# Eight instead of six products by C on GpSimd in a Mamba block with a ternary feed-forward layer, and the steps around them

## The chip, the cores and the metric

One NeuronCore of a Trainium2 chip runs the whole program. The metric is the device time of one execution in microseconds; lower is better. Engines are named as the profile names them: PE is TensorE, DVE is VectorE, ACT is ScalarE, POOL is GpSimd, and SP is the sync engine, which only issues transfers here.

## What is computed

Sixteen rows (the batch) of 512 tokens with 256 channels pass through a selective scan, a layer norm, a feed-forward net and a second layer norm. The part that matters:

```python
xx, res = split(x @ in_w.T)               # 512 inner channels each
xx = silu(causal_conv4(xx) + conv_b)
delta, B, C = split(xx @ xproj_w.T)       # 16 states
delta = softplus(delta @ dt_w.T + dt_b)
dA, dBu = exp(delta * A), delta * B * u
carry = dA[t] * carry + dBu[t]            # the scan over 512 tokens
y[t] = sum over 16 states of carry * C[t]
x1 = layernorm(x + ((y + u * D) * silu(res)) @ out_w.T)
h = silu(x1 @ w1) * (x1 @ w2)
h = gelu(h @ h1); h = gelu(h @ h2)
out = layernorm(x1 + h @ w3)
```

## The kernel before

The channels lie on the 128 partitions in four tiles (DC = 4), the 512 tokens of a row along the free axis. A row has 16 states times 4 channel tiles = 64 scan tiles. Two tiles make a **pair**, so a row has 32 pairs, numbered p = 0 to 31; pair p belongs to state p // 2.

Each engine runs its own list of instructions in order, and semaphores tie the lists together. The order is written by hand as **steps**: one iteration of the main loop has 64 steps s = 0 to 63, and in iteration i four rows are in flight at once: row i is scanned, row i+1 goes through its *front* (input projection, convolution, delta), row i-1 through its *tail* (gates, output projection, first norm, first feed-forward layer, and the hidden layers from step 31 on), and row i-2 through its *end* (the rest of the hidden layers at steps numbered 64 and up, the last layer, second norm, output). Constants at the head of the file say in which step each thing is issued: `T_RES`, `T_GATE`, `T_OUT`, `T_ADD`, `T_STATS` for the tail, `E_W3`, `E_SCALE`, `E_ADD`, `E_STATS` for the end, `F_...` for the front, `B_AT` for the transposes that PE makes for a pair, `HALF_AT`, `GELU_AT` and `SPLIT_AT` for half matrix products, GELUs and splits of the hidden layers, `L1_AT` for the tiles of the first layer, and `EXP_COUNT` for how many tiles of exp(delta * A) ACT makes in a step. A step is no time: engines meet only where a semaphore makes them.

For a pair, PE transposes dB = duT * B into PSUM (`b_pair`, L420). DVE scans at step 2p (`scan_pair`, L792). At step 2p+1 the states are multiplied by C and stored in one of four buffers hC. For most pairs DVE does that from PSUM (`c_pair`, L803). For pairs in `POOL_PAIRS` (rows 1 to 15) or `FIRST_POOL_PAIRS` (row 0), the scan writes hC itself and POOL multiplies in place (`y_pair`, L991); GpSimd has no part in the scan. Then POOL issues the transfer that adds hC to y (L1001). These transfers go in two chains, for even and odd pairs, and each waits for the one before it in its chain. The C rows are loaded by SP for a state at a time into two buffers (`load_c`), when the products two states back are done.

PE starts `b_pair` of pair p when PSUM of pair p-2 is free: after the product by C where DVE makes it, already after the scan where POOL does.

The feed-forward products use a high and a low part: POOL splits each activation tile into both (`split_tile`, L1040 and L1042). The tail's gates are L710 on ACT and L887 on DVE; the sum with x is L894, the scaling of the last layer L923, its sum with x1 L930, and the first layer's gate and product L908 and L915.

Of the kernel before, what the change touches and what calls it, by code (L numbers as in the profile page):

```python
# [37 lines left out]
QUARTERS = 2 * W3_SLOTS  # L38


T_RES = (0, 6, 7, 9)
T_GATE = (2, 5, 8, 11)
T_OUT = (12, 14, 16, 17)
T_ADD = (16, 18)
T_STATS = (17, 18)
T_NORM = 19
T_X1T = (20, 21)
E_W3 = (10, 11, 12, 18)
E_SCALE = (12, 19)
E_ADD = (14, 20)  # L50
E_STATS = (17, 21)
E_NORM = 22
B_AT = (-2, 0, 4, 5, 7, 9, 10, 12, 14, 15, 18, 20, 22, 24, 26, 28, 31, 32, 34, 35, 37, 40, 42, 43, 47, 48, 50, 51,
        54, 56, 58, 61)
L1_AT = (22, 24, 25, 26, 27, 28, 29, 31)
L1_SPLIT_AT = (22, 24, 25, 26, 27, 28, 29, 30)
HALF_AT = (31, 32, 34, 35, 36, 37, 38, 40, 42, 44, 45, 46, 47, 48, 49, 50, 51, 52, 53, 54, 55, 56, 57, 60, 61, 62,
           63, 64, 65, 70, 71, 72)
GELU_AT = (38, 39, 39, 45, 46, 47, 49, 51, 56, 57, 57, 65, 65, 66, 72, 72)
SPLIT_AT = (39, 40, 41, 47, 48, 49, 51, 52, 60, 61, 62, 66, 69, 70, 72, 72)  # L60
F_XX = (30, 32, 34, 36)
FIRST_XX = (30, 31, 32, 33)
F_DBL = 39
F_DBL_OUT = 40
F_BT = 48
F_BT_OUT = 51
F_DT = (40, 41, 43, 46)
F_PLUS = (44, 46, 47, 49)
F_BASE = (41, 43, 46, 50)
F_LOST = (47, 47, 49, 51)  # L70
F_LN = 51
F_DELTA = (53, 53, 53, 53)
F_DELTA_U = (53, 53, 53, 53)
F_Y = (59, 59, 61, 63)
F_DU = (55, 56, 57, 58)
F_XR = 51
SCALE_LEAD = 7

EXP_LEAD, DA_RING = 4, 8
EXP_COUNT = (1, 2, 0, 0, 2, 0, 3, 1, 0, 1, 0, 0, 0, 3, 1, 0, 0, 4, 0, 1, 3, 0, 0, 1, 2, 0, 2, 1, 0, 0, 2, 0, 1, 2,
             1, 0, 2, 3, 1, 0, 2, 1, 3, 0, 1, 0, 0, 0, 3, 2, 0, 0, 0, 2, 3, 0, 0, 0, 1, 0, 0, 2, 3, 1)
EXP_FIRST = EXP_LEAD
EXP_AT = [(EXP_FIRST + sum(EXP_COUNT[:s]), EXP_COUNT[s]) for s in range(TILES)]
PREP_AT = (-30, -27, -25, -24, -20, -12, -7, -5, -3, 2, 5, 12, 16, 17, 18, 20, 23, 26, 30, 33, 38, 39)
# [3 lines left out]
FLAG_AT = 48  # L90
DVE_SLOTS = 12
X_FRONT_AT = 22
OUT_AT = 24
X32 = 4
RAW = 4
HC_SLOTS = 4
POOL_PAIRS = (1, 8, 11, 13, 16, 17)
FIRST_POOL_PAIRS = (0, 3, 4, 9, 14, 16, 17, 18, 25, 27, 28)
SUM_AT = tuple(min(63, 2 * p + (5 if p in FIRST_POOL_PAIRS else 3)) for p in range(0, PAIRS, 2))

# [21 lines left out]
def build(nc, x, xT_in, in_wT, chan, xproj_wT, dt_wT, out_wT, ffn_w, ffn_s, w3_s, ident_in, out):  # L122
# [3 lines left out]
    with ExitStack() as ctx:  # L126
# [171 lines left out]
        def _(sp):  # L298
# [42 lines left out]
            def entry_step(e):  # L341

                used = e - RING
                if used < 0:
                    return E_W3[-1]
                if used < FIRST_HALF:
                    return L1_AT[used]
                return HALF_AT[used - FIRST_HALF]

# [64 lines left out]
        def _(pe):  # L414
# [80 lines left out]
            def tail_step(r, par, s):  # L495
                if s in T_RES:
                    c = T_RES.index(s)
                    if c:
# [7 lines left out]
                    in_proj(misc_ps, DC + c, xT_tail).then_inc(pe_res, 1)  # L506
                if s in T_OUT:
                    t = T_OUT.index(s)
                    if t == 0:
# [82 lines left out]
            def iteration(i, par, full):  # L592
                (scan, _), (front, fpar), (tail, tpar), (end, _) = rows(i, par)
                for s in range(TILES):
                    if scan is not None and s in B_AT:
                        b_pair(scan, B_AT.index(s))
                    if front is not None and s - TILES in B_AT:
                        b_pair(front, B_AT.index(s - TILES))
                    if i == 0 and s in SUM_AT:
                        sum_pair(2 * SUM_AT.index(s))  # L600
                    if i == 0 and s == FLAG_AT + 1:
                        pe.wait_ge(low_summed, 1)
                        nc.tensor.matmul(ffn_ps[0][0:1, 0:1], low_sum[:], ones[:], start=True, stop=True
                                         ).then_inc(low_total, 1)
                    if end is not None and s in E_W3:
                        w3_tile(end, E_W3.index(s), full)
                    if tail is not None:
# [6 lines left out]
                    if tail is not None:  # L614
                        if s in L1_AT:
                            l1_tile(tail, L1_AT.index(s), full)
                        if s in HALF_AT:
                            half_tile(tail, HALF_AT.index(s), full)

# [12 lines left out]
        def _(act):  # L632
# [71 lines left out]
            def tail_step(r, s):  # L704
                if s in T_GATE:
                    c = T_GATE.index(s)
                    act.wait_ge(pe_res, r * DC + (c + 1))
# [52 lines left out]
        def _(dve):  # L760
# [122 lines left out]
            def tail_step(r, par, s):  # L883
                if s in T_GATE:
                    c = T_GATE.index(s)
                    dve.wait_ge(v_tanh, r * DC + (c + 1))
# [32 lines left out]
            def end_step(f, par, s):  # L919
                if s in E_SCALE:  # L920
                    k = E_SCALE.index(s)
                    dve.wait_ge(pe_w3, f * TT + 2 * (k + 1))
# [3 lines left out]
                                            ).then_inc(w3_scaled, 1)  # L926
                if s in E_ADD:
                    k = E_ADD.index(s)
                    dve.wait_ge(w3_scaled, f * 2 + (k + 1))
                    nc.vector.tensor_tensor(out_st[:, 2 * k:2 * k + 2, :], out_st[:, 2 * k:2 * k + 2, :],  # L930
                                            x1[:, par, 2 * k:2 * k + 2, :], ALU.add).then_inc(z2_ready, 1)
                if s in E_STATS:
                    statistics(1, out_st, f, E_STATS.index(s), z2_ready)
                if s == E_NORM:
# [47 lines left out]
        def _(pool):  # L982
# [69 lines left out]
            def iteration(i, par):  # L1052
                (scan, spar), (front, fpar), (tail, tpar), (end, _) = rows(i, par)
                for s in range(TILES):
                    if scan is not None and s % 2:
                        y_pair(scan, spar, s // 2)
                    if tail is not None:
                        if s - 1 in T_GATE:
                            gate_tile(tail, tpar, T_GATE.index(s - 1))
                        if s == T_STATS[-1]:  # L1060
                            rstd_of(0, tail)
                        ffn_step(tail, s)
                    if end is not None:
                        if s == E_STATS[-1]:
                            rstd_of(1, end)
# [62 lines left out]
```

## Time and profile before

| what | value |
| --- | --- |
| median of 3 runs | 2681.95 us (2679.81 to 2683.85) |
| the profiled execution | 2681.34 us |
| its span in the trace | 2679.5 us |
| DVE busy | 2413.4 us, 90% of the span |
| PE busy | 2423.5 us, 90% (ends are modelled) |
| ACT busy | 2101.1 us, 78% |
| POOL busy | 1605.8 us, 60% |

The 1.84 us between span and time lie around the program. Matrix products overlap in PE's pipeline, so PE's busy share is not its share of peak speed. In the middle of the run the iterations follow each other at an even pace, so a difference in one iteration counts as often as it repeats. In a timeline row, the bracket at the end says how long the engine stood idle before the instruction, and which engine's work ended that; a row without bracket began as soon as its engine was free.

### The profile page before, as it was taken

To read this page: it belongs to the slowest core of one execution; us is meant where nothing else is said; L and a number is where in the kernel's file an instruction comes from. 1 tells how busy PE (TensorE), PEld (TensorE's weight loads), DVE (VectorE), ACT (ScalarE), POOL (GpSimd) and SP (SyncE) were. 2 spreads that over 40 slices of the span, in tenths; PEclk is the share of its full clock that TensorE was granted. 3 is DMA by queue.
4 is the path that set the end of the run, shared out by engine and by line. 5 is a ranking of instruction groups with operands and counts; after the bars stand their busy time and mean duration, and the time that the engine had idled before them with its cause. 6 is when DMAs were issued, how large, how long until landed. Compare 5 with 4: busy or idle time off the path is not lost. (4 is left out here: it accounts for less than half of the span.)

```text
span 2679.5 us, 36236 instructions
## 1 busy us (share of the span) xinstructions
PE 2423.5 (90%) x12098; PEld 1844.0 (69%) x12098; DVE 2413.4 (90%) x2388; ACT 2101.1 (78%) x3225; POOL 1605.8 (60%) x1561
## 2 busy tenths in 40 slices
PE   5677999989999998989999899998989899898988
PEld 2445776867767686776767677686767768576777
DVE  6899999999999999999999999999999999999730
ACT  5886988969788896978879697887969789696611
POOL 1335567665756666566566656656665675657554
PEclk7889999999999999999999999999999999999999
DMA  7758999989899898989989898998989899898933
GB/s 250 217 138 197 223 216 223 228 211 237 206 225 225 214 231 209 238 204 223 223 219 232 206 236 200 228 224 213 243 205 229 204 231 223 212 241 201 254 105 114
DMA packets 224491, 573.26 MB, mean 214 GB/s; under 512 B 25664, under 2 KB 26048, under 8 KB 223824
## 3 DMA queue, kind: packets, MB, share of 16 engines
q0 software_dynamic: 71424, 260.08, 51.9%
q1 hardware_dynamic: 152880, 310.84, 35.3%
q8 instruction: 99, 1.62, 0.2%
q14 instruction: 88, 0.72, 0.1%
HBM read 301.86 MB, written 20.45 MB: 120 GB/s over the span
## 5 line engine op out<-in xcount | busy, mean ns | idle before, releaser
L792 DVE TENSOR_TENSOR_SCAN scan_ps<-dA,scan_ps 128x1024 f32<-128x1024 f32 x411 | 939.7, 2286 | 62.4 <-PE scan_ps L420 61.5
L1001 POOL DMA_DIRECT2D y<-hC x496 | 441.6, 890 | 714.8 <-DVE hC L803 544.6
L651 ACT ACTIVATE dB<-duT,bT 128x512 f32<-128x512 f32 x1024 | 711.0, 712 | 50.9 <-PE scan_ps L420 50.8
L539 PE MATMUL ffn_ps<-hb_hi,ring 128*128 128x512 f32 x1536 | 655.2, 427 | 36.5 <-DVE gate L908 17.4
L642 ACT ACTIVATE dA<-delta,ch 128x512 f32<-128x512 f32 (+1 forms) x1024 | 681.3, 711 | 0.9
L420 PE MATMUL scan_ps<-ident,dB 128*128 128x128 f32 x4096 | 556.7, 282 | 76.8 <-DVE hC L803 60.9
L420 PEld LDWEIGHTS scan_ps<-ident,dB 128*128 128x128 f32 x4096 | 488.1, 145 | 193.7 <-issue 67.2
L539 PE MATMUL ffn_ps<-hb_lo,ring 128*128 128x512 f32 x1536 | 611.2, 398 | 0.0
L803 DVE TENSOR_TENSOR hC<-scan_ps,c_rows_sb 128x1024 f32<-128x1024 f32 x411 | 501.0, 1219 | 42.6 <-DMA c_rows_sb<-c_rows 5.7
L539 PE MATMUL ffn_ps<-ha_hi,ring 128*128 128x512 f32 x1024 | 428.0, 418 | 25.9 <-POOL ha_lo L1042 25.7
L539 PE MATMUL ffn_ps<-ha_lo,ring 128*128 128x512 f32 x1024 | 402.5, 393 | 0.0
L539 PEld LDWEIGHTS ffn_ps<-hb_hi,ring 128*128 128x128 f32 x1536 | 295.6, 192 | 131.7 <-DVE gate L908 39.1
L1042 POOL TENSOR_TENSOR ha_lo<-x,ha_hi 128x512 fp32r<-128x512 f32 x256 | 329.1, 1285 | 21.2
L539 PEld LDWEIGHTS ffn_ps<-hb_lo,ring 128*128 128x128 f32 x1536 | 296.2, 193 | 63.8 <-issue 10.7
L991 POOL TENSOR_TENSOR hC<-hC,c_rows_sb 128x1024 f32<-128x1024 f32 x101 | 252.5, 2500 | 70.0 <-DVE hC L792 69.9
L539 PEld LDWEIGHTS ffn_ps<-ha_hi,ring 128*128 128x128 f32 x1024 | 193.2, 189 | 112.9 <-issue 38.5
L1040 POOL CAST ha_hi<-x 128x512 fp32r<-128x512 f32 x256 | 195.0, 762 | 109.3 <-DVE x L915 93.1
L719 ACT ACTIVATE x<-ffn_ps,fs 128x512 f32<-128x512 f32 x256 | 170.0, 687 | 83.8 <-PE ffn_ps L539 82.7
L792 DVE TENSOR_TENSOR_SCAN hC<-dA,scan_ps 128x1024 f32<-128x1024 f32 x101 | 229.8, 2277 | 3.3 <-ACT dA L642 3.3
L539 PEld LDWEIGHTS ffn_ps<-ha_lo,ring 128*128 128x128 f32 x1024 | 193.9, 189 | 41.8 <-issue 6.7
L728 ACT ACTIVATE gate<-ffn_ps,fs 128x512 f32<-128x512 f32 x128 | 87.8, 686 | 150.5 <-PE ffn_ps L539 150.5
L1042 POOL TENSOR_TENSOR hb_lo<-x,hb_hi 128x512 fp32r<-128x512 f32 x128 | 168.3, 1315 | 10.6
(103 smaller groups left out, 3172.2 us busy)
## 6 DMA issues: line engine op xcount, KB each, us to landing
y<-hC POOLq DMA_DIRECT2D x496, 512.0 KB, 6.3
ring<-rounded_weights SPq DMA_DIRECT2D x704, 256.0 KB, 4.9
c_rows_sb<-c_rows SPq DMA_DIRECT2D x256, 256.0 KB, 5.0
x<-ffn_w SPq DMA_DIRECT2D x22, 512.0 KB, 6.1
rounded_weights<-ffn_w SPq DMA_DIRECT2D x22, 512.0 KB, 6.4
xt<-x_chan SPq DMA_DIRECT2D x16, 512.0 KB, 3.9
xt<-x_tok SPq DMA_DIRECT2D x16, 512.0 KB, 5.5
out_st<-x_chan SPq DMA_DIRECT2D x16, 512.0 KB, 4.9
```

Of the source, the lines that this page charges most:

```text
L420: mm = nc.tensor.transpose(dst[:, j * P:(j + 1) * P], src(j), ident[:])
L539: mm = nc.tensor.matmul(dst, w, a, start=(first and n == 0), stop=(last and n == len(steps) - 1))
L642: nc.scalar.activation(dA[:, s % DA_RING, s % 2:], delta2[:, par, c, s % 2:], ACT.Exp, scale=a_neg[:, c, n:n + 1]).then_inc(dA_ready, 1)
L651: nc.scalar.activation(dB[:, n % 2, t, :], duT[:, t, :], ACT.Copy, scale=bT2[:, par, t, n:n + 1]).then_inc(dB_ready, 1)
L719: nc.scalar.activation(x32[:, i % X32, :], ffn_ps[(2 * HC + i) % 3][:], ACT.Gelu, scale=fs[:, 2 + i // HC, i % HC:i % HC + 1]).then_inc(ge ...
L728: nc.scalar.activation(gate[:, o % 2, :], ffn_ps[2 * o % 3][:], ACT.Tanh, scale=s1_half[:, o:o + 1]).then_inc(l1_tanh, 1)
L792: nc.vector.tensor_tensor_scan(states, dA[:, a:a + 2, :].rearrange("p a l -> p (a l)"), b, 0.0, ALU.mult, ALU.add).then_inc(scan_done, 1)
L803: nc.vector.tensor_tensor(hC[:, (r * PAIRS + p) % HC_SLOTS], scan_ps[:, h:h + 2, :], c_rows[:, n % 2].unsqueeze(1).to_broadcast([P, 2, SEQ ...
L991: nc.gpsimd.tensor_tensor(hC[:, slot], hC[:, slot], c_rows[:, n % 2].unsqueeze(1).to_broadcast([P, 2, SEQ]), ALU.mult).then_inc(hC_pool, 1)
L1001: pool.dma_start(y2[:, par, c:c + 2, :], hC[:, slot], accum_op=ALU.add).then_inc(y_added[p % 2], 16)
L1040: nc.gpsimd.tensor_copy(hi[:, i % HC, :], x32[:, i % X32, :]).then_inc(ffn_hi, 1)
L1042: nc.gpsimd.tensor_tensor(lo[:, i % HC, :], x32[:, i % X32, :], hi[:, i % HC, :].bitcast(F32), ALU.subtract).then_inc(ffn_lo, 1)
```

## The change

`POOL_PAIRS` gains pairs 7 and 10, so in rows 1 to 15 POOL makes eight products by C of 32 instead of six. Beside that, 16 tables of steps change: several entries by one or two steps, `F_PLUS[0]` and `E_STATS[0]` by two, `F_Y` by up to four, and `EXP_COUNT` as a whole (its sum stays 64). No function changes.

```diff
-T_RES = (0, 6, 7, 9)
-T_GATE = (2, 5, 8, 11)
-T_OUT = (12, 14, 16, 17)
+T_RES = (0, 5, 7, 9)
+T_GATE = (2, 5, 8, 10)
+T_OUT = (13, 14, 15, 16)
-E_W3 = (10, 11, 12, 18)
-E_SCALE = (12, 19)
-E_ADD = (14, 20)
-E_STATS = (17, 21)
+E_W3 = (10, 12, 13, 18)
+E_SCALE = (13, 19)
+E_ADD = (15, 20)
+E_STATS = (15, 21)
-B_AT = (-2, 0, 4, 5, 7, 9, 10, 12, 14, 15, 18, 20, 22, 24, 26, 28, 31, 32, 34, 35, 37, 40, 42, 43, 47, 48, 50, 51,
+B_AT = (-2, 0, 3, 5, 7, 8, 10, 12, 14, 15, 18, 20, 22, 25, 26, 28, 31, 32, 34, 35, 37, 40, 41, 42, 47, 48, 50, 51,
         54, 56, 58, 61)
-L1_AT = (22, 24, 25, 26, 27, 28, 29, 31)
+L1_AT = (23, 24, 25, 26, 27, 28, 30, 31)
-HALF_AT = (31, 32, 34, 35, 36, 37, 38, 40, 42, 44, 45, 46, 47, 48, 49, 50, 51, 52, 53, 54, 55, 56, 57, 60, 61, 62,
-           63, 64, 65, 70, 71, 72)
-GELU_AT = (38, 39, 39, 45, 46, 47, 49, 51, 56, 57, 57, 65, 65, 66, 72, 72)
-SPLIT_AT = (39, 40, 41, 47, 48, 49, 51, 52, 60, 61, 62, 66, 69, 70, 72, 72)
+HALF_AT = (31, 32, 34, 35, 36, 37, 38, 40, 41, 44, 45, 46, 47, 48, 49, 50, 51, 52, 53, 54, 55, 56, 57, 59, 61, 62,
+           63, 66, 67, 70, 71, 72)
+GELU_AT = (38, 39, 39, 45, 47, 47, 49, 50, 56, 57, 57, 65, 65, 66, 72, 73)
+SPLIT_AT = (38, 40, 40, 48, 48, 50, 51, 51, 57, 58, 63, 66, 68, 70, 71, 72)
-F_BT_OUT = 51
-F_DT = (40, 41, 43, 46)
-F_PLUS = (44, 46, 47, 49)
-F_BASE = (41, 43, 46, 50)
-F_LOST = (47, 47, 49, 51)
-F_LN = 51
-F_DELTA = (53, 53, 53, 53)
-F_DELTA_U = (53, 53, 53, 53)
-F_Y = (59, 59, 61, 63)
-F_DU = (55, 56, 57, 58)
+F_BT_OUT = 49
+F_DT = (40, 41, 43, 47)
+F_PLUS = (42, 45, 46, 49)
+F_BASE = (41, 44, 45, 49)
+F_LOST = (45, 47, 49, 51)
+F_LN = 52
+F_DELTA = (54, 54, 54, 54)
+F_DELTA_U = (54, 54, 54, 54)
+F_Y = (55, 56, 60, 62)
+F_DU = (55, 56, 57, 59)
-EXP_COUNT = (1, 2, 0, 0, 2, 0, 3, 1, 0, 1, 0, 0, 0, 3, 1, 0, 0, 4, 0, 1, 3, 0, 0, 1, 2, 0, 2, 1, 0, 0, 2, 0, 1, 2,
-             1, 0, 2, 3, 1, 0, 2, 1, 3, 0, 1, 0, 0, 0, 3, 2, 0, 0, 0, 2, 3, 0, 0, 0, 1, 0, 0, 2, 3, 1)
+EXP_COUNT = (0, 3, 0, 0, 2, 0, 1, 2, 2, 0, 0, 2, 1, 2, 1, 0, 0, 0, 2, 1, 4, 0, 0, 0, 3, 1, 0, 1, 0, 2, 1, 0, 1, 0,
+             3, 0, 3, 1, 2, 0, 2, 1, 2, 1, 0, 0, 0, 0, 0, 5, 0, 0, 0, 1, 4, 0, 0, 0, 2, 0, 2, 0, 0, 3)
-OUT_AT = 24
+OUT_AT = 26
-POOL_PAIRS = (1, 8, 11, 13, 16, 17)
+POOL_PAIRS = (1, 7, 8, 10, 11, 13, 16, 17)
```

## Rows read from the trace of the kernel before

**Rows 1.** The page: busy time, share of the span, number of instructions.

```profile
PE 2423.5 (90%) x12098; PEld 1844.0 (69%) x12098; DVE 2413.4 (90%) x2388; ACT 2101.1 (78%) x3225; POOL 1605.8 (60%) x1561
```

**Rows 2.** One iteration's window: busy us of each engine, granted clock, DMA share.

```profile
2219.00:2376.35 157.35, 146.96 (x753) 112.80 (x752) 150.19 (x149) 131.26 (x202) 100.31 (x98) 0.99 0.92 221
```

**Rows 3.** DVE's timeline: the same instruction in two iterations (start, us, instruction).

```profile
1112.45 2.49 DVE L855 TENSOR_TENSOR du<-y,delta 128x512 f32<-128x512 f32 x4
...
1269.82 2.48 DVE L855 TENSOR_TENSOR du<-y,delta 128x512 f32<-128x512 f32 x4
```

**Rows 4.** DVE's timeline, same iteration: waits that end at PE or ACT.

```profile
1142.27 2.30 DVE L792 TENSOR_TENSOR_SCAN scan_ps<-dA,scan_ps 128x1024 f32<-128x1024 f32 x1 [0.78 <-PE scan_ps L420]
...
1146.34 0.69 DVE L887 SCALAR_TENSOR_TENSOR gate<-gate,misc_ps 128x512 f32<-128x512 f32 x1 [0.42 <-ACT gate L710]
...
1242.58 2.30 DVE L792 TENSOR_TENSOR_SCAN scan_ps<-dA,scan_ps 128x1024 f32<-128x1024 f32 x1 [1.51 <-PE scan_ps L420]
```

**Rows 5.** PE's timeline, same iteration.

```profile
1168.02 3.62 PE L514 MATMUL ffn_ps<-outw,y 128*128 128x256 f32 x16
...
1175.85 1.09 PE L420 MATMUL scan_ps<-ident,dB 128*128 128x128 f32 x8 [1.43 <-DVE hC L803]
...
1215.19 0.50 PE L539 MATMUL ffn_ps<-ha_hi,ring 128*128 128x512 f32 x1 [1.52 <-POOL ha_lo L1042]
```

**Rows 6.** Groups by line: busy us, mean ns; idle before and releasers.

```profile
L803 DVE TENSOR_TENSOR hC<-scan_ps,c_rows_sb 128x1024 f32<-128x1024 f32 x411 | 501.0, 1219 | 42.6 <-DMA c_rows_sb<-c_rows 5.7 <-DMA y<-hC 4.3 <-DVE scan_ps L792 1.0
L991 POOL TENSOR_TENSOR hC<-hC,c_rows_sb 128x1024 f32<-128x1024 f32 x101 | 252.5, 2500 | 70.0 <-DVE hC L792 69.9
```

**Rows 7.** DVE's timeline around pairs 7 and 10.

```profile
1164.75 0.67 DVE L930 TENSOR_TENSOR out_st<-out_st,x 128x512 f32<-128x512 f32 x1
1165.35 1.21 DVE L803 TENSOR_TENSOR hC<-scan_ps,c_rows_sb 128x1024 f32<-128x1024 f32 x1
1166.47 2.27 DVE L792 TENSOR_TENSOR_SCAN hC<-dA,scan_ps 128x1024 f32<-128x1024 f32 x1
...
1172.75 0.68 DVE L894 TENSOR_TENSOR xt<-ffn_ps,xt 128x512 f32<-128x512 f32 x1
...
1175.71 0.68 DVE L923 TENSOR_TENSOR out_st<-ffn_ps,w3s 128x512 f32<-128x512 f32 x1
...
1180.98 1.21 DVE L803 TENSOR_TENSOR hC<-scan_ps,c_rows_sb 128x1024 f32<-128x1024 f32 x1
1182.11 0.74 DVE L869 BATCH_NORM_STATS2 stats<-out_st 128x6 f32<-128x256 f32 x2
```

**Rows 8.** POOL's timeline, same iteration.

```profile
1166.86 0.87 POOL L1001 DMA_DIRECT2D y<-hC  x1 [3.03 <-DVE hC L803]
...
1176.46 0.98 POOL L1001 DMA_DIRECT2D y<-hC  x1 [0.38 <-DMA y<-hC]
1182.49 0.85 POOL L1001 DMA_DIRECT2D y<-hC  x1 [5.05 <-DVE hC L803]
...
1213.18 0.61 POOL L1040 CAST ha_hi<-x 128x512 fp32r<-128x512 f32 x1 [1.73 <-DVE x L915]
...
1220.31 2.76 POOL L991 TENSOR_TENSOR hC<-hC,c_rows_sb 128x1024 f32<-128x1024 f32 x1 [0.74 <-DVE hC L792]
...
1291.53 1.29 POOL L1042 TENSOR_TENSOR ha_lo<-x,ha_hi 128x512 fp32r<-128x512 f32 x1
```

**Rows 9.** DVE's timeline: a pair of POOL's, and an operation beside POOL's.

```profile
1217.94 2.28 DVE L792 TENSOR_TENSOR_SCAN hC<-dA,scan_ps 128x1024 f32<-128x1024 f32 x1
1220.13 0.67 DVE L824 SCALAR_TENSOR_TENSOR y<-delta,y 128x512 f32<-128x512 f32 x1
...
1291.58 1.53 DVE L861 TENSOR_SCALAR y<-y,ch 128x512 f32<-128x512 f32 x1
```

**Rows 10.** One line's instructions: durations in ns, lowest, median, highest.

```profile
L861 DVE TENSOR_SCALAR y<-y,ch x64: 473/479/1545, 49.3 to 2394.0; 128x512 f32<-128x512 f32 x64
```

## The prediction

> **What bounds the kernel now.** I read the page first, for shares: DVE and PE are both at 90%, ACT at 78%, POOL at 60% [rows 1]. Two engines at 90% don't say which one sets the pace, so I went on to one iteration. In DVE's timeline the same instruction returns after 1269.82 - 1112.45 = 157.37 us [rows 3], and in a window of that length DVE is busy for 150.2 us, PE for 147.0, ACT for 131.3, POOL for 100.3, the transfers for 0.92 of the time at a granted clock of 0.99 [rows 2]. So an iteration has 7 us in which DVE isn't computing and 10 in which PE isn't; no engine bounds it by itself. The time is a cycle that runs through several, and the reader has to find where it passes from one to the next. I took the timelines of all four engines for one iteration and looked for idle times.
>
> DVE waits for PE or ACT only from step 42 on, and at the start of the next iteration: 1.51 us at the scan of pair 22, 0.78 at that of pair 2, 0.42 at the second gate [rows 4]. From the second gate at 1146.34 to the scan of pair 21 it has no bracket: there its own work is the path. PE has the opposite picture. Its waits lie between 1175.85 and 1215.19, the last of 1.52 us on a split of POOL's [rows 5], which had itself stood idle for DVE's product of the first layer (L915) [rows 8]. After that PE runs on with one wait of half a microsecond until the third part of the output projection and the last part of w3 in the next iteration. So the cycle is: DVE from the second gate to the last tile of the first layer, 67 us; POOL's split; PE through the hidden layers; ACT, which in the same stretch has no idle time until it makes that gate, for which DVE waits the 0.42 [rows 4]; and DVE again. Work taken from DVE between 1146 and 1213 shortens the cycle; work taken elsewhere needn't.
>
> **The change part by part.**
>
> *The products of pairs 7 and 10.* Both lie within that stretch. From the start of the product of pair 7 to the next start DVE spends 1166.47 - 1165.35 = 1.12 us, and for pair 10 1182.11 - 1180.98 = 1.13 [rows 7]. That is 2.25 us an iteration (the mean duration of 1.219 [rows 6] counts an overlap of 0.1 with the next instruction twice). It happens in the scans of rows 1 to 15: 15 x 2.25 = 33.8 us.
>
> *What POOL takes over.* Two products of 2.50 us [rows 6] and about 0.3 until the transfer can be issued: 5.6 us on an engine that is idle for 57. Where they fall: for pair 7, POOL stood idle for 3.03 us before the transfer at 1166.86, for pair 10 5.05 before the one at 1182.49 [rows 8]. The second hides entirely. The first ends about 1 us later than the old product did, at about 1167.9, and the odd chain of transfers with it: the one of pair 9 already waited 0.38 for that of pair 7 [rows 8], so it goes to about 1177.4. Behind it stand POOL's product of pair 10 (its scan ends at 1178.8 then) and, behind that, the second norm's root, needed by DVE at about 1184.1 and done by 1183.8. So 0.3 us is left of that cover; if the landing is 1 us later still, it costs DVE 0.7. I take 0, with 0.7 as the other end. SP's load of C for pairs 12 and 13 waits for pair 9 as before, that for 10 and 11 now for POOL, 1 us later than the 1166.5 at which DVE was done with pair 7, and 11 us ahead of its use; ring loads stand behind it, and none was urgent there.
>
> *PE's side of the same pairs.* `b_pair` of pairs 9 and 12 now waits for a scan, not a product. That only helps: a wait on the product of pair 10 goes. `b_pair` of pair 11 stood 1.43 us for the product of pair 9 [rows 5], which is earlier by pair 7's 1.12. Here is the limit of the gain: PE ends the third and fourth part of the output projection at 1171.64 and DVE uses them at 1172.75; the last part of w3 ends near 1174.4 and DVE takes it at 1175.71 [rows 5, 7]. The slack is 1.1 to 1.3 us, and taking out pair 7 uses 1.12 of it. So the product of pair 7 may give its 1.12 in full, with nothing over.
>
> *Moved steps on DVE in this stretch.* `E_SCALE` to 13 puts the product of pair 6 directly behind its scan, `L1_AT[6]` to 30 puts work between scan and product of pair 15. A product right behind its scan starts 2.42 us after the scan's start, other work 2.20: +0.22 and -0.22. `E_STATS` to 15 puts statistics right behind their sum, about +0.1 from the same pattern (starts 0.70 apart rather than 0.58). `T_GATE[3]` a step earlier finds ACT ready by 0.5 us. Sum 0.1, so 2.15 from DVE.
>
> *Moved steps on PE and ACT.* `b_pair` 22 passes the second delta projection, and takes up to 1.05 of DVE's wait of 1.51; `b_pair` 2 passes a half product of 1.85 and takes the 0.78 [rows 4]. Both waits lie outside DVE's part of the cycle: the second gate is still made by ACT at the same place, so they turn into a longer wait there. The fourth delta projection goes behind a half product, which gives ACT its GELU up to 1.05 earlier and the exponential behind it 0.2 later; ACT's chain to the gate gains 0 to 1.0. Against that, `F_PLUS[0]` at 42 comes before ACT's exponential is done (0.6 of wait), `F_DELTA` behind a scan of 2.3 us uses up most of the 1.9 us that PE's transposes had, and the new `EXP_COUNT` has one to two tiles more lead where DVE's old lead was none (steps 12, 16 and 60), one where it had four (48). Tables and work counts stay equal. I take +0.1 us of gain, with -1.5 and +2.3 (both of DVE's waits on PE in full) as the ends. The same moves in iterations -1, 0, 16 and 17 I take as 0, with 3 us to either side.
>
> *A shared resource.* DVE operations on data in SBUF and POOL's operations slow each other: L861 took 1.53 us when it began beside POOL's L1042, against a median of 0.48 [rows 8 to 10], so it waited until POOL was done. In the new order `E_ADD` (L930) comes right behind the scans of both new pairs, and POOL's product starts when the scan ends. The nearest row is pair 17: DVE's next operation began 2.19 us after the scan's start, POOL's product 2.37 after it and took 2.76 instead of the median of 2.4: DVE was first and POOL paid [rows 8, 9]. I take 0 for DVE, and 0.4 on POOL.
>
> The Trainium skill, SBUF — State Buffer, section Who interferes with whom, says that a DVE instruction with two SBUF inputs and a GpSimd one that reads SBUF take one port in turn, and that whichever starts first keeps it for the whole instruction. The trace agrees (1.53 against 0.48). Its page Perfetto Trace Analysis, section Optimizing Scalar/DVE Operations, warns that moving work between these two engines might not help. By that rule at its worst the sum would be that of the third rival below. The scan and the products that go have one input in PSUM, and by the first page they don't contend.
>
> *Sum.* 2.15 + 0.1 = 2.25 us in each of 15 iterations, 33.8 us. From the profiled execution's 2681.34 that makes 2647.6; the median of the runs is 0.6 above it, so 2648.
>
> **The rivals.**
>
> *More (2614 to 2640).* PE's and ACT's new order shortens their part of the cycle as well. For it speaks that the two waits on PE, 2.29 us, are just where `b_pair` moved. Against it, the output projection's slack of 1.1 is used up. In full 15 x (2.25 + 2.3) = 68 us: 2614.
>
> *Less (2658 to 2676).* PE's chain doesn't follow: DVE arrives 1.1 us earlier at the output projection and finds it late, or transfers of the odd chain hold POOL. Then only pair 10 pays, 15 x 1.13 = 17 us: 2665. For it speaks the small slack, and 0.92 of transfer time that becomes 0.94.
>
> *Slower.* POOL's product takes the port before L930. L930 then waits for the whole product, 2.4 us. For one pair that is 2.4 - 2.25, +2 us in all; for both 4.8 - 2.25 = 2.55 an iteration, 38 us: 2720. It is decided by 0.18 us, the distance of 2.37 and 2.19; should POOL see the end of the scan earlier than DVE can start its next instruction, it goes this way.
>
> *No change (2676.6 to 2687.3).* The products go from DVE, but what they leave is wait: the cycle closes through PE alone. Against it: PE is idle for 10 us an iteration, and all of that hangs on DVE.
>
> **How the numbers follow.** The forecast, 2640 to 2658, gets 0.48; more 0.16; less 0.23; no change 0.05; slower 0.08. Two in a thousand of the time, 5.4 us, is what a measurement of this kernel can tell from nothing, since the runs shown spread over 4 us. So faster is 0.87, the same 0.05, slower 0.08. The range of 2626 to 2671 takes in the forecast, most of "less", which reaches past the 2665 of one pair alone, and the upper part of "more".
>
> **What the profile after should show.** L803 x381 and L991 x131; 147.9 us of DVE in a window of an iteration; L855 returning after 155.1 us; pair 7's gap on DVE closed, with L930 at 0.67 and POOL's product at up to 2.8; DVE's wait at the scan of pair 22 under 0.5, and a longer one at the second gate; PE's 1.43 before `b_pair` 11 nearly gone. I'm wrong if L930 takes over 1 us, if DVE waits at L894 or L923 for PE, or if the return time is under 154 or over 156.

## The result and the profile after

The changed kernel takes 2709.36 us (median of 4 runs, 2706.68 to 2711.5) beside 2680.89 for the kernel before in the same job: ratio 1.0105, 95% interval 1.0092 to 1.0118. It is 28 us slower where 34 us of gain were forecast. The profiled execution took 2711.5 us, its span 2709.7.

The page of the changed kernel, busy time of the engines [rows 1]:

```profile
PE 2429.5 (90%) x12098; PEld 1839.3 (68%) x12098; DVE 2390.9 (88%) x2358; ACT 2111.3 (78%) x3225; POOL 1689.7 (62%) x1591
```

Its groups of the two products [rows 6]:

```profile
L803 DVE TENSOR_TENSOR hC<-scan_ps,c_rows_sb 128x1024 f32<-128x1024 f32 x381 | 464.4, 1219 | 33.9 <-DMA c_rows_sb<-c_rows 6.9 <-DMA y<-hC 3.9 <-DVE scan_ps L792 1.0
...
L991 POOL TENSOR_TENSOR hC<-hC,c_rows_sb 128x1024 f32<-128x1024 f32 x131 | 337.1, 2574 | 107.3 <-DVE hC L792 97.9 <-DMA c_rows_sb<-c_rows 8.5 <-DMA y<-hC 0.7
```

The work went where it should: 30 products of 1.219 us left DVE, 36.6 us. But DVE's busy time fell by only 22.5, so other instructions of DVE take more. DVE's timeline, the same instruction in two iterations [rows 3]:

```profile
1130.44 0.69 DVE L855 TENSOR_TENSOR du<-y,delta 128x512 f32<-128x512 f32 x1
...
1290.55 0.69 DVE L855 TENSOR_TENSOR du<-y,delta 128x512 f32<-128x512 f32 x1
```

This iteration takes 160.1 us instead of 157.4. It is one of the longer ones: from the third iteration on the changed kernel's last 158.5 to 160.7 us, 159.8 in the mean of 13, against 157.5 before. That is 2.3 us each and 30 in all, which is the difference between the two profiled executions. I split the iteration at the second gate and at PE's first half product behind the last first-layer tile. DVE's part, second gate to the start of the last L915, went from 65.93 us (1212.27 - 1146.34) to 64.3 to 64.8: it gained 1.2 to 1.6, not 2.15. The rest of the cycle, PE's half products to the next second gate, went from 88.5 to between 91.2 and 93.0. The loss is there, and the reader finds where it starts in the timelines around step 49. DVE of the changed kernel:

```profile
1228.51 0.75 DVE L915 SCALAR_TENSOR_TENSOR x<-gate,fs,ffn_ps 128x512 f32<-128x512 f32 x1
...
1269.62 2.30 DVE L792 TENSOR_TENSOR_SCAN scan_ps<-dA,scan_ps 128x1024 f32<-128x1024 f32 x1 [1.38 <-PE scan_ps L420]
1272.05 1.23 DVE L803 TENSOR_TENSOR hC<-scan_ps,c_rows_sb 128x1024 f32<-128x1024 f32 x1
1274.57 2.05 DVE L838 TENSOR_SCALAR out_st<-du 128x512 f32<-128x512 f32 x1 [1.30 <-PE misc_ps L475]
1276.55 1.78 DVE L844 SCALAR_TENSOR_TENSOR delta<-gate,delta 128x512 f32<-128x512 f32 x1
```

The same stretch of the kernel before:

```profile
1254.18 2.29 DVE L792 TENSOR_TENSOR_SCAN scan_ps<-dA,scan_ps 128x1024 f32<-128x1024 f32 x1 [0.75 <-PE scan_ps L420]
1256.61 1.23 DVE L803 TENSOR_TENSOR hC<-scan_ps,c_rows_sb 128x1024 f32<-128x1024 f32 x1
1257.87 0.43 DVE L838 TENSOR_SCALAR out_st<-du 128x512 f32<-128x512 f32 x1
1258.21 0.69 DVE L844 SCALAR_TENSOR_TENSOR delta<-gate,delta 128x512 f32<-128x512 f32 x1
```

And POOL of the changed kernel at that moment:

```profile
1273.58 0.88 POOL L1001 DMA_DIRECT2D y<-hC  x1 [0.86 <-DVE hC L803]
1274.19 1.59 POOL L1009 TENSOR_TENSOR delta<-delta,du 128x512 f32<-128x512 f32 x1
1275.43 0.90 POOL L1040 CAST hb_hi<-x 128x512 fp32r<-128x512 f32 x1
1276.41 1.36 POOL L1042 TENSOR_TENSOR hb_lo<-x,hb_hi 128x512 fp32r<-128x512 f32 x1
1282.18 0.88 POOL L1001 DMA_DIRECT2D y<-hC  x1 [4.41 <-DVE hC L803]
1282.78 0.90 POOL L1040 CAST hb_hi<-x 128x512 fp32r<-128x512 f32 x1
```

Step 49 holds the product of pair 24 (L803) and then the fourth "1 + e" of the softplus (L838); L844 is the softplus step behind it. DVE comes to L838 after a wait of 1.30 us for PE's transposes L475. By then POOL has begun its base step (L1009, its own part of the softplus), its split follows, and L838 and L844 take 2.05 + 1.78 us instead of 0.43 + 0.69: 2.71 us more for the same work. DVE's next product comes later by that, POOL's transfer waits 4.41 us for it with the next two splits queued behind it, and PE waits for those. PE's timeline:

```profile
1281.94 1.09 PE L420 MATMUL scan_ps<-ident,dB 128*128 128x128 f32 x8 [0.90 <-DVE hC L803]
...
1287.01 0.50 PE L539 MATMUL ffn_ps<-hb_hi,ring 128*128 128x512 f32 x1 [2.13 <-POOL hb_lo L1042]
```

In the waits of the whole run, PE's L539 stood 37.8 us for `hb_lo`, against 14.0 before, both times in 16 waits. This reading is only a chain of neighbours in time until something in it is taken out. The total of PE's wait alone turns out to be a poor measure of the loss: two runs below have the one without the other.

### The profile page after: what moved, and what is told of

Same layout as the page of the kernel before. It is cut to its first block and busy times, and to the rows that moved or that the text cites. A ratio compares the mean times of both kernels' runs of the same rounds, so it can differ in the third digit from the quotient of the medians.

```text
span 2709.7 us, 36236 instructions
## 1 busy us (share of the span) xinstructions
PE 2429.5 (90%) x12098; PEld 1839.3 (68%) x12098; DVE 2390.9 (88%) x2358; ACT 2111.3 (78%) x3225; POOL 1689.7 (62%) x1591
## 5 line engine op out<-in xcount | busy, mean ns | idle before, releaser
L792 DVE TENSOR_TENSOR_SCAN scan_ps<-dA,scan_ps 128x1024 f32<-128x1024 f32 x381 | 871.2, 2287 | 66.9 <-PE scan_ps L420 48.1
L539 PE MATMUL ffn_ps<-hb_hi,ring 128*128 128x512 f32 x1536 | 667.4, 435 | 69.8 <-POOL hb_lo L1042 37.8
L420 PE MATMUL scan_ps<-ident,dB 128*128 128x128 f32 x4096 | 550.4, 279 | 72.0 <-DVE hC L803 56.6
L539 PE MATMUL ffn_ps<-hb_lo,ring 128*128 128x512 f32 x1536 | 614.8, 400 | 0.0
L420 PEld LDWEIGHTS scan_ps<-ident,dB 128*128 128x128 f32 x4096 | 484.0, 143 | 177.7 <-DVE hC L803 54.4
L803 DVE TENSOR_TENSOR hC<-scan_ps,c_rows_sb 128x1024 f32<-128x1024 f32 x381 | 464.4, 1219 | 33.9 <-DMA c_rows_sb<-c_rows 6.9
L539 PE MATMUL ffn_ps<-ha_hi,ring 128*128 128x512 f32 x1024 | 427.5, 417 | 28.0 <-POOL ha_lo L1042 25.6
L539 PEld LDWEIGHTS ffn_ps<-hb_hi,ring 128*128 128x128 f32 x1536 | 297.5, 194 | 171.7 <-DVE gate L908 52.9
L991 POOL TENSOR_TENSOR hC<-hC,c_rows_sb 128x1024 f32<-128x1024 f32 x131 | 337.1, 2574 | 107.3 <-DVE hC L792 97.9
L539 PE MATMUL ffn_ps<-ha_lo,ring 128*128 128x512 f32 x1024 | 401.7, 392 | 0.0
L539 PEld LDWEIGHTS ffn_ps<-hb_lo,ring 128*128 128x128 f32 x1536 | 298.0, 194 | 66.5 <-issue 14.1
L792 DVE TENSOR_TENSOR_SCAN hC<-dA,scan_ps 128x1024 f32<-128x1024 f32 x131 | 298.3, 2278 | 5.3 <-PE scan_ps L420 5.3
L539 PEld LDWEIGHTS ffn_ps<-ha_hi,ring 128*128 128x128 f32 x1024 | 192.3, 188 | 131.7 <-issue 39.5
L539 PEld LDWEIGHTS ffn_ps<-ha_lo,ring 128*128 128x128 f32 x1024 | 193.0, 188 | 41.9 <-issue 6.7
```

The lines of the kernel that those rows point to most:

```text
L420: mm = nc.tensor.transpose(dst[:, j * P:(j + 1) * P], src(j), ident[:])
L539: mm = nc.tensor.matmul(dst, w, a, start=(first and n == 0), stop=(last and n == len(steps) - 1))
L792: nc.vector.tensor_tensor_scan(states, dA[:, a:a + 2, :].rearrange("p a l -> p (a l)"), b, 0.0, ALU.mult, ALU.add).then_inc(scan_done, 1)
L803: nc.vector.tensor_tensor(hC[:, (r * PAIRS + p) % HC_SLOTS], scan_ps[:, h:h + 2, :], c_rows[:, n % 2].unsqueeze(1).to_broadcast([P, 2, SEQ ...
L991: nc.gpsimd.tensor_tensor(hC[:, slot], hC[:, slot], c_rows[:, n % 2].unsqueeze(1).to_broadcast([P, 2, SEQ]), ALU.mult).then_inc(hC_pool, 1)
```

## The experiments

Each ratio is to the kernel before on the same chip; its 95% interval stands behind it.

**Pairs without moves.** The kernel before with

```diff
-POOL_PAIRS = (1, 8, 11, 13, 16, 17)
+POOL_PAIRS = (1, 7, 8, 10, 11, 13, 16, 17)
```

> The kernel before with the new POOL_PAIRS alone; all step tables as before. Theory A (the moved steps cost the time, the two products on GpSimd gain it): the stretch from the second gate to the last first-layer tile shrinks by 1.6 to 2.2 us an iteration as in the profile after, nothing else changes, 15 iterations: 2648 to 2657 us. Theory B (the two products themselves cost it, through GpSimd's queue and the shared port): 2700 us or more. Theory C (half and half): about 2680.

2665.98 us, 0.9935 (0.9919 to 0.9952). The products pay, but 17 us and not 34, which none of the three theories had.

**Moves without pairs.** The changed kernel with the six pairs of before.

> The kernel after with the old six POOL_PAIRS; all step tables as after. Theory A: the gain of the two products is missing, 24 to 33 us over the 2709 of after: 2733 to 2742. Theory B: the cost goes with the two products: 2675 to 2690. Theory C: about 2709.

2723.29 us, 1.016 (1.0141 to 1.018). The moves alone cost 43 us, the pairs give 15 of it back, fewer than the 24 to 33 of theory A.

**The softplus tables as before.** The changed kernel with

```diff
-F_BT_OUT = 49
-F_DT = (40, 41, 43, 47)
-F_PLUS = (42, 45, 46, 49)
-F_BASE = (41, 44, 45, 49)
-F_LOST = (45, 47, 49, 51)
+F_BT_OUT = 51
+F_DT = (40, 41, 43, 46)
+F_PLUS = (44, 46, 47, 49)
+F_BASE = (41, 43, 46, 50)
+F_LOST = (47, 47, 49, 51)
```

> The kernel after with F_DT, F_PLUS, F_BASE, F_LOST and F_BT_OUT as before (delta projection and softplus up to the logarithm), all else as after. Theory A1 (the loss starts at step 49, where DVE waits 1.3 us for the B transposes, then 2.7 us for GpSimd's port, and so holds GpSimd's split and PE's hidden layer): DVE's 1.30 wait on L475 is gone, L838 and L844 there are back under 1.0, PE's wait on hb_lo falls from 2.13 to about 0.6, and 2.5 to 3.1 us an iteration come back: 2662 to 2672. Theory A2 (the loss comes from the exponentials or from the hidden layers' steps): 2700 to 2712.

2677.39 us, 0.9974 (0.9961 to 0.9986): 35 us of the moves' cost are in these five tables; the time is 5 us above the range of A1.

**The exponentials as before.** The changed kernel with the old `EXP_COUNT`.

> The kernel after with EXP_COUNT as before, all else as after. Theory A1: the wait at step 49 stays, little changes: 2700 to 2712. Theory A2 with the exponentials as the cause (five in step 49 ahead of a GELU, DVE's wait of 1.8 us for dA at a scan behind step 58): 2675 to 2690.

2768.25 us, 1.0315 (1.0298 to 1.0332). Neither expectation had this: 56 us more than the changed kernel. With the old table the fourth gate waits 2.15 us for ACT, where the changed kernel has no wait, and DVE's part of the cycle is 68.2 us instead of 64.3 to 64.8. PE's transposes L475, too, stand 1.33 us for ACT's L684 in the middle iterations, and L838 2.7 us for them. So the new table doesn't cost time among the other new ones, it saves some; whether it would cost any by itself isn't shown.

**One entry.** The changed kernel with only the fourth delta projection back:

```diff
-F_DT = (40, 41, 43, 47)
+F_DT = (40, 41, 43, 46)
```

> The changed kernel with the fourth delta projection back in front of its half product (F_DT[3] = 46). Theory P (step 49: a late projection starts it, the port makes it large): DVE's wait of 1.30 us before the fourth 1 + e falls by the 0.46 that PE's transposes come earlier, so DVE starts before POOL's base step and L838 takes about 0.45 instead of 2.05; L844 may still stand behind POOL once. 15 x (0.46 + 0.5 to 1.6) gives 2678 to 2695. Rival Q (only the lateness counts): 15 x 0.46 = 7 us, 2702. Rival R (the placement of the fourth projection is no part of the cause): 2706 to 2712.

2675.7 us, 0.9982 (0.9972 to 0.9992). That is (1.0105 - 0.9982) x 2681 = 33 us from one number; the expected gain of 15 to 31 was still a little low. In the 13 middle iterations the mean is 157.1 us against 159.8, which is 2.7, the 2.71 by which L838 and L844 were stretched. DVE's timeline of this run:

```profile
1204.78 0.75 DVE L915 SCALAR_TENSOR_TENSOR x<-gate,fs,ffn_ps 128x512 f32<-128x512 f32 x1
...
1247.17 2.30 DVE L792 TENSOR_TENSOR_SCAN scan_ps<-dA,scan_ps 128x1024 f32<-128x1024 f32 x1 [2.65 <-PE scan_ps L420]
1249.60 1.23 DVE L803 TENSOR_TENSOR hC<-scan_ps,c_rows_sb 128x1024 f32<-128x1024 f32 x1
1250.86 0.43 DVE L838 TENSOR_SCALAR out_st<-du 128x512 f32<-128x512 f32 x1
1251.20 0.69 DVE L844 SCALAR_TENSOR_TENSOR delta<-gate,delta 128x512 f32<-128x512 f32 x1
```

Here the reader is to add the waits. DVE stands 2.65 us for PE before the scan and none at L838; in the changed kernel it stands 1.38 + 1.30 = 2.68. The projection only moved a wait from one side of the scan to the other. And it doesn't make DVE late. Counted from the start of the last L915, L838 starts after 1250.86 - 1204.78 = 46.08 us here and after 1274.57 - 1228.51 = 46.06 in the changed kernel. PE's timeline shows why, of this run first (the fourth projection is L484, L420 here is `b_pair` of pair 24):

```profile
1243.03 1.12 PE L484 MATMUL misc_ps<-out_st,dtw 16*128 16x512 f32 x2
...
1246.03 1.03 PE L420 MATMUL scan_ps<-ident,dB 128*128 128x128 f32 x8
...
1249.70 1.06 PE L475 MATMUL misc_ps<-ident,out_st 16*128 16x16 f32 x8
```

and of the changed kernel:

```profile
1268.48 1.03 PE L420 MATMUL scan_ps<-ident,dB 128*128 128x128 f32 x8
1269.44 1.12 PE L484 MATMUL misc_ps<-out_st,dtw 16*128 16x512 f32 x2
...
1273.42 1.06 PE L475 MATMUL misc_ps<-ident,out_st 16*128 16x16 f32 x8
```

The moved projection goes behind a half product and also behind `b_pair` of pair 24. The transposes L475 stand behind all of these in either order and begin 44.92 and 44.91 us after that L915: the 0.46 us that I expected to come back doesn't. (L475 does begin 0.47 us later than in the kernel before, after 44.91 us instead of 44.44, but in the run with both repairs, below, it begins after 44.9 us too.) But `b_pair` of pair 24 begins after 39.97 us instead of 41.25, the scan and the product come as much earlier, and so does what POOL has behind that product, its transfer and its base step: after 45.68 us instead of 46.96. POOL's base step of this run:

```profile
1251.74 1.59 POOL L1009 TENSOR_TENSOR delta<-delta,du 128x512 f32<-128x512 f32 x1
```

So L838 stays where it was, and POOL's base step passes from 0.88 us behind its start to 0.38 ahead of it. PE's wait for `hb_lo` in this run is 14.1 us in all, as before the change.

**The base step behind the split.** The changed kernel, `b_pair` of pair 24 still ahead of the projection, with

```diff
-F_BASE = (41, 44, 45, 49)
+F_BASE = (41, 44, 45, 50)
```

> The changed kernel with POOL's fourth base step behind the split again (F_BASE[3] = 50), all else as changed; PE's transposes stay 0.46 us late. Theory P: L838 no longer meets POOL's 1.59 us base step, but L844 may meet the split's second half; of the 2.7 us of stretching 1 to 1.5 go, 15 x 1 to 1.5 gives 2687 to 2694. Rival Q (the stretching costs nothing, the lateness does): 2706 to 2712.

2688.56 us, 1.0025 (1.0015 to 1.0035): 21 us less than the changed kernel. DVE's timeline:

```profile
1260.53 0.80 DVE L838 TENSOR_SCALAR out_st<-du 128x512 f32<-128x512 f32 x1 [1.30 <-PE misc_ps L475]
1261.25 1.78 DVE L844 SCALAR_TENSOR_TENSOR delta<-gate,delta 128x512 f32<-128x512 f32 x1
```

The wait of 1.30 is the same, and L838 has lost 1.25 of its 2.05 us; over the 14 iterations that have this wait it is 17.5 us of the 21. L838 now begins beside the first half of POOL's split, L844 still takes 1.78 beside its second. So it is the meeting with POOL that costs, nearly microsecond for microsecond, and not the wait for L475. The rival that the stretching costs nothing is out. The edit also brings the split forward, but POOL only stands idle behind it, for 2.71 us before the transfer that waits for DVE's next product, 4.41 in the changed kernel. PE's wait for `hb_lo` is still 36.1 us in all; what is gone in the iteration read is the 0.90 us for which PE stood before its L420.

**The softplus tables alone.** The kernel before with the five tables of the change.

> The kernel before with only the five softplus tables of the change (F_DT, F_PLUS, F_BASE, F_LOST, F_BT_OUT), pairs and all else old. Theory P: they cost as much alone as they gave back when undone, about 32 us, 2705 to 2722, with the fourth L838 or L844 over 1.5 us beside POOL. Rival S (they cost only together with the new exponentials or half products): within 10 us of before, 2675 to 2693.

2721.2 us, 1.0149 (1.0132 to 1.0166). They cost 40 us in the other surroundings too, but not by the same way, so this run doesn't repeat the finding. With the old `EXP_COUNT` L475 itself stands 1.37 us for ACT's L684, L838 waits 2.73 us for it and takes only 0.72, and L844 takes 1.77. PE's wait for `hb_lo` is 14.4 us in all, as in the kernel before.

**All tables of the front as before.** The changed kernel with the softplus five and `F_LN`, `F_DELTA`, `F_DELTA_U`, `F_Y` and `F_DU` of before.

> The changed kernel with all ten tables of the front as before (the softplus five and F_LN, F_DELTA, F_DELTA_U, F_Y, F_DU). With the softplus five alone it was 2677.4, the pairs alone 2666.0. Theory T (the remaining 11 us lie in the later part of the front): 2664 to 2670. Rival U (they lie in the tail's and end's tables, the half products and the exponentials): 2674 to 2680.

2676.28 us, 0.9978 (0.9968 to 0.9987). No better than the one entry: the later part of the front, with its projection of delta behind a scan, costs nothing. 12 us above the pairs alone are left, as rival U had it.

**Half products, GELUs and splits as before too.** The same with `HALF_AT`, `GELU_AT` and `SPLIT_AT` of before.

> The changed kernel with the ten tables of the front and HALF_AT, GELU_AT and SPLIT_AT of before. With the front's alone it was 2676.3, with the pairs alone 2666.0. Theory X (the 10 us between them lie in the order of half products, GELUs and splits, which is where PE lost 1 us an iteration): 2664 to 2669. Rival Y (they lie in EXP_COUNT, B_AT or the tail's and end's tables): 2673 to 2679.

2664.74 us, 0.9931 (0.9918 to 0.9945): the 12 us are in these three tables. In the middle iterations of this run DVE's second gate waits 0.23 to 0.30 us for ACT's gate, in the run before it 1.29; from PE's first half product to that gate it is 88.9 us instead of 89.8 to 90.2. The rest (`EXP_COUNT`, `B_AT`, the tail's and the end's tables) has no measurable cost in these surroundings.

**The two repairs together.** The changed kernel with `F_DT[3] = 46` and those three tables of before.

> The changed kernel with F_DT[3] = 46 and HALF_AT, GELU_AT and SPLIT_AT of before, all else as changed. Theory Z (the change's loss has two places only, step 49 with 33 us and the half products with 11, and they add): 2709.4 - 33.7 - 11.5 = 2664, range 2661 to 2669. Rival (with the other softplus moves kept, the half products' order of before meets DVE late again): 2672 to 2680.

2667.49 us, 0.9944 (0.9926 to 0.9961). The two losses add, within the interval.

**Pair 10 alone, pair 7 alone.** The kernel before with one product more on POOL.

```diff
-POOL_PAIRS = (1, 8, 11, 13, 16, 17)
+POOL_PAIRS = (1, 8, 10, 11, 13, 16, 17)
```

> The kernel before with pair 10 alone moved to POOL. DVE loses 1.13 us of work behind pair 8's scan, so that scan's wait of 0.46 shouldn't appear; the wait of 0.7 for hb_hi may take part. Theory V: 15 x 0.6 to 1.13, 2666 to 2673. Rival W (the hb_hi wait takes what there is): 2674 to 2680.

```diff
-POOL_PAIRS = (1, 8, 11, 13, 16, 17)
+POOL_PAIRS = (1, 7, 8, 11, 13, 16, 17)
```

> The kernel before with pair 7 alone moved to POOL. Its 1.12 us lie ahead of pair 8's scan, where 0.46 waits for ACT. Theory V: 15 x (1.12 - 0.46) = 10 us, 2670 to 2674. Rival W (the rest is lost again at hb_hi): 2678 to 2683.

Pair 10: 2677.67 us, 0.9979 (0.997 to 0.9988), 6 us, in the range of rival W. Pair 7: 2672.69 us, 0.9963 (0.9949 to 0.9977), 10 us, as theory V had it. Each should have given 17 by the prediction. Where the rest of pair 10's went is seen in DVE's timeline of its run:

```profile
1179.44 0.69 DVE L903 TENSOR_TENSOR hb_lo<-misc_ps,hb_hi 128x512 fp32r<-128x512 f32 x1
1180.04 0.74 DVE L869 BATCH_NORM_STATS2 stats<-out_st 128x6 f32<-128x256 f32 x2
...
1181.97 0.69 DVE L903 TENSOR_TENSOR hb_lo<-misc_ps,hb_hi 128x512 fp32r<-128x512 f32 x1 [0.70 <-ACT hb_hi L714]
```

Between the two L903 runs a chain through three engines: the first frees PSUM, PE transposes, ACT makes the next `hb_hi`, DVE goes on. Before, pair 10's product stood between them and covered it (1180.98 in [rows 7]). By the waits of each run, L903 stood for `hb_hi` 17 times for 11.3 us in all with pair 10 moved, 17 times for 11.7 with both, but 3 times for 1.7 with pair 7 alone and 3 times for 2.2 before. Pair 7's loss is a wait for ACT's exponentials at the scan of pair 8, DVE's timeline with both pairs moved:

```profile
1158.48 2.29 DVE L792 TENSOR_TENSOR_SCAN hC<-dA,scan_ps 128x1024 f32<-128x1024 f32 x1 [0.46 <-ACT dA L642]
```

2.25 - 0.70 - 0.46 = 1.09 us, times 15 is 16 us; the pairs alone gained 17. The two waits vary from one iteration to the next, the second between 0.21 and 0.85 us, so this is an estimate.

**Two exponentials a step earlier.** The pairs alone, and in `EXP_COUNT`

```diff
-EXP_COUNT = (1, 2, 0, 0, 2, 0, 3, 1, 0, 1, 0, 0, 0, 3, 1, 0, 0, 4, 0, 1, 3, 0, 0, 1, 2, 0, 2, 1, 0, 0, 2, 0, 1, 2,
+EXP_COUNT = (1, 2, 0, 0, 2, 0, 3, 1, 0, 1, 0, 0, 0, 3, 1, 0, 2, 2, 0, 1, 3, 0, 0, 1, 2, 0, 2, 1, 0, 0, 2, 0, 1, 2,
```

> The kernel before with the new POOL_PAIRS and two exponentials moved from step 17 to step 16, where DVE waited 0.46 us for ACT at the scan of pair 8. Theory V (that wait is part of what the pairs' 2.25 us lost): it goes, 15 x 0.4 = 6 us below the pairs alone, 2658 to 2662. Rival W (DVE waits longer for ACT's hb_hi instead, or the gate comes later): 2664 to 2668.

2667.63 us, 0.9937 (0.9923 to 0.995): nothing gained, as the rival had it. The scan of pair 8 still starts 0.37 us late in the iteration read, with no releaser to be seen, and DVE now waits 0.51 for ACT's gate of the first layer (L908). Whether ACT's order or its mere amount of work holds pair 7's other half stays open.

**Pair 12 instead of pair 10.** Is there a place in DVE's part of the cycle where a product pays in full?

```diff
-POOL_PAIRS = (1, 8, 11, 13, 16, 17)
+POOL_PAIRS = (1, 7, 8, 11, 12, 13, 16, 17)
```

> The kernel before with pairs 7 and 12 on POOL instead of 7 and 10. Pair 12's product stands among the first layer's tiles, where in the run with the pairs alone DVE has no wait, but POOL works through its splits from 1185.24 to 1203.17 with no idle time and has only 1.70 us left before the last split. Theory K (POOL's backlog): 2.7 us more on POOL there delay the last split by about 1 us and eat pair 12's 1.13: 2668 to 2682, not below pair 7 alone (2672.7) by more than 5. Rival (each product taken from DVE there pays in full): 2672.7 - 17 = 2656, range 2652 to 2660.

2717.31 us, 1.0139 (1.0118 to 1.016): 47 us worse than pair 7 alone, far outside either expectation. POOL now works through its list of splits without idle time, and ends the last one 4.6 us after DVE's last L915 (1225.95 to 1230.54). PE's timeline:

```profile
1224.62 1.98 PE L425 MATMUL misc_ps<-xt,inw 128*128 128x512 f32 x4 [0.74 <-DVE y L818]
1230.59 0.80 PE L539 MATMUL ffn_ps<-ha_hi,ring 128*128 128x512 f32 x1 [3.98 <-POOL ha_lo L1042]
1231.19 0.63 PE L539 MATMUL ffn_ps<-ha_lo,ring 128*128 128x512 f32 x1
...
1235.88 0.66 PE L425 MATMUL misc_ps<-xt,inw 128*128 128x512 f32 x1
```

and its windows (start:end, length, busy time of PE, weight load, DVE, ACT and POOL with their counts, granted clock, DMA share, GB/s):

```profile
1226.00:1228.00 2.00, 0.61 (x2) 0.00 (x0) 2.00 (x1) 2.00 (x4) 1.92 (x3) 1.00 1.02 268
1228.00:1230.00 2.00, 0.00 (x0) 0.00 (x0) 1.96 (x4) 0.96 (x2) 1.92 (x3) 0.79 1.12 350
1230.00:1232.00 2.00, 1.41 (x3) 1.16 (x4) 1.97 (x3) 1.01 (x2) 2.00 (x3) 0.50 1.02 215
```

With pair 7 alone the same wait is:

```profile
1206.88 0.50 PE L539 MATMUL ffn_ps<-ha_hi,ring 128*128 128x512 f32 x1 [1.52 <-POOL ha_lo L1042]
...
1209.77 1.98 PE L425 MATMUL misc_ps<-xt,inw 128*128 128x512 f32 x4
```

The wait is 2.46 us longer, and the granted clock falls to 0.50, the lower of TensorE's two levels, while PE stands. From the end of the wait to the next projection PE then takes 1235.88 - 1230.59 = 5.29 us instead of 2.89. Together 4.9 us, less DVE's 1.13: an estimate of 3.7 an iteration, where 47 / 15 = 3.1 were measured. Three of the 14 middle iterations have no such loss, their part from L915 to the second gate is 91.4 to 91.6 us instead of 95.4 to 97.1. My expectation had the backlog, but put it at 1 us, and it didn't have the clock.

## Why the prediction was wrong

The figures add up within their intervals, which reach 0.001 to 0.002 to either side. As ratios to the kernel before: the pairs -0.0065, the fourth delta projection with what it met at step 49 +0.0123, the three tables of the half products +0.0047; sum +0.0105, which is what was measured. That it agrees to the last digit is luck: taken between the one entry and both repairs, the three tables cost 0.0038 instead of 0.0047.

**The step that failed** is "Moved steps on PE and ACT", in the sentence on the fourth delta projection. I costed its going behind a half product by what it does to ACT, "0 to 1.0" of gain, and took +0.1 in all, with -1.5 as the lower end; it cost 33 us, 2.7 in each middle iteration. The sentence leaves out that the projection also goes behind `b_pair` of pair 24, and what that sets free. The product of pair 24 comes 1.28 us earlier, and with it POOL's base step. DVE gains nothing from its early product, because L838 waits for PE's transposes L475 by a semaphore that stands in the code, and these don't move. The row that told it was there, in PE's timeline of the kernel before:

```profile
1256.71 1.06 PE L475 MATMUL misc_ps<-ident,out_st 16*128 16x16 f32 x8
```

The transposes ended at 1257.77 and L838 began at 1257.87, right behind its product (1256.61 + 1.23 = 1257.84). Without a bracket it looks as if L838 followed its product only, but the transposes had ended just 0.07 us before it: a product that comes 1.28 us earlier buys a wait of 1.30. The order of the two engines was decided in the meantime. My expectations for the one entry and for the base step blamed late transposes; the gain came, the reason given for it was wrong.

**The resource** was the one I had named, in the wrong place. I put the rule on the shared port on L930, and there everything was as forecast: L930 took 0.67 us behind both new pairs, POOL's products 2.66 and 2.71. Behind pair 10 it was as close as forecast, L930 at 1197.03 and POOL's product at 1197.20; behind pair 7 a transfer of POOL's came between. The collision came some 80 us later, between DVE's L838 and a moved POOL instruction (`F_BASE[3]`, which I put at nothing without a reason). Either repair shows that it takes both moves: the base step at 49 costs nothing measurable when the projection is at 46, and 21 of the 33 us go when it is at 50. The Trainium skill, SBUF — State Buffer, section Who interferes with whom, also lists tensor_scalar among the operations that can take the shared pair, and says that the order of issue decides who is blocked. The trace agrees with both: L838, a tensor_scalar, took 2.05 us behind POOL and 0.43 ahead of it. The row that I gave for the rule on two inputs, L861, is a tensor_scalar with one as well; a row for two inputs is L844, 1.78 us behind POOL against 0.69.

**The products of pairs 7 and 10** were the second step. Counts, durations and place were right (x381, x131, 1.12 and 1.13 us off DVE), and POOL took them without harm. But "2.15 from DVE" supposed that DVE had nothing to wait for in that stretch because it showed no bracket. It had none because the two products filled the time: pair 10's covered the chain between the two L903, pair 7's ran while ACT caught up. By the two waits the term is 1.1 us instead of 2.15, by the time of the run 17.4 / 15 = 1.2. The rival "less" gave 2665 and the pairs alone took 2666, though its reason was wrong: neither the output projection did it (L894 has no wait in the middle iterations there, and 0.15 us in the changed kernel, which is one of the signs I had named for being wrong) nor the chain of transfers (L803 waited 2.1 us in all for one, 4.3 before), and both pairs pay a part. That the sum of that rival came out is luck.

**The half products** are the third. I hadn't costed the moves in `HALF_AT`, `GELU_AT` and `SPLIT_AT` beyond the one beside the delta projection. That they hold 12 us is shown. They reach DVE as a longer wait for ACT's second gate, 1.29 us instead of 0.23 to 0.30, and at least 0.9 us of the cycle in every middle iteration of the two traces; which of the three holds ACT up isn't shown.

**What held.** The cycle itself, and several of the signs. The wait at the scan of pair 22 is gone, the one at the second gate has grown from 0.42 to 1.29 us, and `b_pair` of pair 11 waits 0.38 us instead of 1.43. `F_DELTA` behind a scan and the tail's moves have no cost that can be measured. Why the old `EXP_COUNT` costs as much as 56 us among the new tables is only read from the waits named above; no run takes them apart.

The best versions are the pairs without the moves, the changed kernel with both repairs, and the one with the front's ten and those three tables of before: 2665 to 2667 us, 0.6 to 0.7% faster than before and 1.5 to 1.6% faster than the changed kernel.

## What to carry to other kernels

An engine without idle time in a stretch isn't shown to be the bound there: before taking an instruction out, look at what its neighbours on both sides would wait for, and how late that is. When an instruction is moved back, list what it lets pass, not only what it holds up, and follow what comes earlier on every engine behind it. Then look at the engine that shares a port: has its instruction passed one that it used to follow? An instruction that comes earlier may gain nothing, because the next one waits for something else, and still decide which of two engines comes first.

## What the runs showed of the hardware

- Two short DVE instructions of 0.43 and 0.69 us took 2.05 and 1.78 when each began just after a POOL instruction on SBUF data. Whether POOL's base step began 0.88 us behind L838 or 0.38 ahead of it, with the same total of DVE's waits (2.65 against 2.68 us), made 33 us of the run.
- TensorE's clock can make a wait cost more than its length. A wait of 3.98 us ended at a granted clock of 0.50, and the next 2.89 us of work took 5.29; after a wait of 1.52 the clock was still 1.00.
- The same level sets the wait between the two L903. With pair 10 moved, in the iteration shown above:

```profile
1176.00:1178.00 2.00, 1.12 (x5) 0.71 (x4) 2.00 (x4) 0.04 (x1) 0.51 (x1) 0.70 0.85 229
1178.00:1180.00 2.00, 0.00 (x0) 0.00 (x0) 2.00 (x3) 1.16 (x2) 0.96 (x1) 0.50 0.95 261
```

PE's four transposes between the two L903 take 1.11 us here instead of the 0.66 in the iteration of the kernel before: 0.45 of the 0.70 us for which L903 waits. In every middle iteration of that run it is one or the other, 1.11 or 1.12 us and a wait of 0.70 or 0.71, or 0.65 or 0.66 us and a wait of 0.24 or 0.25. Moving pair 10 isn't what lowers the clock: the kernel before has transposes of both durations too, and its product covers either. Nor does PE's idle time just before them decide. It is 2.72 us before fast and before slow ones, and 2.26 or 2.27 only where the four transposes ahead of it were slow already. What decides isn't shown.
